# A recurrence with added filling products in every half step and in its head, and a head with its columns on a semaphore of their own

## The reference

```python
ms = jnp.mean(jnp.square(tokens), axis=-1, keepdims=True)
x = tokens * jax.lax.rsqrt(ms + EPS) * norm_w
x = x.reshape(B, T, H, D)            # 8, 256, 16, 8
a_t = jnp.tanh(a)                    # 16, 64, 64
def step(state, x_t):
    state = jnp.tanh(jnp.einsum('bhs,hst->bht', state, a_t) + jnp.einsum('bhd,hds->bhs', x_t, b))
    mixed = jnp.einsum('bhs,hsd->bhd', state, c) + skip[None] * x_t
    return (state, mixed)
_, outs = jax.lax.scan(step, state0, moveaxis(x, 1, 0))
return tokens + outs @ w_out.T + b_out
```

## Time and profile before

| | |
|---|---|
| time, median of 3 runs | 1920.63 us (1919.22 to 1922.42) |
| span of the profiled execution | 1914.6 us |
| mean granted clock of PE | 0.883 |
| PE busy | 1691.7 us (88%) |
| DVE busy | 1499.7 us (78%) |
| ACT busy | 1262.2 us (66%) |
| POOL busy | 453.8 us (24%) |

### The profile page before, as it was taken

One profiled execution on the slowest core, in us unless ns is written; L12 is line 12 of the kernel. 1 busy time (PEld: TensorE's weight loads), 2 busy tenths in 40 slices (PEclk: granted clock), 3 DMA queues, 4 the chain that ended last, 5 costly groups with the idle time before them and its releaser, 6 DMA issues. The chain is left out here.

```text
span 1914.6 us, 45800 instructions
## 1 busy us (share of the span) xinstructions
PE 1691.7 (88%) x16657; PEld 1055.0 (55%) x16662; DVE 1499.7 (78%) x3630; ACT 1262.2 (66%) x3371; POOL 453.8 (24%) x581
## 2 busy tenths in 40 slices
PE   5999977969869999966679999999969999999786
PEld 4999973437634444444444444444436666566453
DVE  4444457968779999978779999999967877788675
ACT  5666646856646655567558888888856666566675
POOL 1000001318411111110012222222214344435333
PEclk7555568969979999978789999999979999999998
DMA  3200005500024444200056666666610000000000
GB/s 80 91 4 4 4 13 196 190 1 2 2 98 157 156 163 169 106 1 1 1 206 234 224 222 231 233 226 222 230 61 23 12 11 23 23 2 1 1 11 15
DMA packets 52464, 174.80 MB, mean 91 GB/s; under 512 B 7376, under 2 KB 32976, under 8 KB 34896
## 3 DMA queue, kind: packets, MB, share of 16 engines
q1 hardware_dynamic: 51152, 170.69, 24.8%
q10 hardware_dynamic: 1152, 1.90, 0.3%
HBM read 168.05 MB, written 2.95 MB: 89 GB/s over the span
## 5 line engine op out<-in xcount | busy, mean ns | idle before, releaser
L864 DVE TENSOR_TENSOR ps<-ps,m_comb 128x512 f32<-128x512 f32 x520 | 363.0, 698 | 24.7 <-DMA m_comb<-m_shares 7.4
L849 DVE TENSOR_TENSOR m_hwlo<-ps,m_hwhi 128x512 f16<-128x512 f32 x520 | 353.6, 680 | 0.3
L825 ACT ACTIVATE m_hwhi<-ps 128x512 f16<-128x512 f32 x520 | 308.7, 594 | 20.9 <-DVE ps L864 19.5
L831 ACT ACTIVATE ps<-ps 128x512 f32<-128x512 f32 x388 | 225.8, 582 | 80.5 <-PE ps L781 80.4
L754 POOL CAST m_whi<-m_stage 128x256 f16<-128x256 f32 (+1 forms) x130 | 55.5, 427 | 899.9 <-PE ps L787 633.6
L781 PE MATMUL ps<-x_hi,m_whi 128*128 128x512 f16 x652 | 249.3, 382 | 11.1 <-DVE m_hwlo L849 6.6
L781 PE MATMUL ps<-x_lo,m_whi 128*128 128x512 f16 x652 | 249.1, 382 | 0.0
L781 PE MATMUL ps<-x_hi,m_wlo 128*128 128x512 f16 x652 | 248.9, 382 | 0.0
L463 DVE TENSOR_TENSOR rn_s_lo<-rn_s_full,rn_s_hi 128x32 f16<-128x32 f32 x512 | 98.5, 192 | 131.8 <-ACT rn_s_full L420 131.8
L787 PE MATMUL ps<-m_hwhi,m_whi 128*128 128x512 f16 x520 | 197.5, 380 | 0.3 <-DVE m_hwlo L849 0.2
L787 PE MATMUL ps<-m_hwlo,m_whi 128*128 128x512 f16 x520 | 197.3, 379 | 0.0
(11 more groups left out here) (456 smaller groups left out, 3973.2 us busy)
## 6 DMA issues: line engine op xcount, KB each, us to landing
m_comb<-m_shares SPq DMA_DIRECT2D x128, 1024.0 KB, 5.1
m_stage<-in_m_w SPq DMA_DIRECT2D x97, 128.0 KB, 4.5
m_stage<-in_m_w SPq DMA_DIRECT2D x33, 192.0 KB, 4.6
kept_lj_w<-in_lj_w SPq DMA_DIRECT2D x6, 1024.0 KB, 4.9
kept_lq_w<-in_lq_w SPq DMA_DIRECT2D x1, 1600.0 KB, 8.0
kept_la_w<-in_la_w SPq DMA_DIRECT2D x1, 1280.0 KB, 5.6
rn_rows<-in_L_attn_rows SPq DMA_DIRECT2D x4, 256.0 KB, 4.3
rn_xs<-rn_xn_hi SPq DMA_DIRECT2D x32, 32.0 KB, 1.9
```

Source lines behind the costliest of these rows:

```text
L825: nc.scalar.activation(hw_hi[:, k % HB, :], weighted(k), ACT.Copy).then_inc(hi_done, 1)
L831: nc.scalar.activation(acted(k), ps[:, 4, :] if gated else bank(k), func).then_inc(act_done, 1)
L849: nc.vector.tensor_tensor(hw_lo[:, k % HB, :], weighted(k), hw_hi[:, k % HB, :], ALU.subtract)\
L864: nc.vector.tensor_tensor(weighted(k), bank(k), comb[:, s, n * QW:(n + 1) * QW], ALU.mult)\
```

## The change

- The load of `cols` goes ahead of the later groups of rows and gets the semaphore `load_cols`. `base` on DVE and the scaling on ACT wait for it and no longer for w_out.
- ACT asks for the table of the square root at its start and for that of the tanh right after the square root. It scales group 0, then makes `at_hi` itself (a tanh to fp16) and `a_t`, then scales groups 1 to 3 to f32 only.
- POOL waits until the rows are normalised, then does what it did, and then the high and low parts of groups 1 to 3 of xn. DVE keeps the low part of group 0 and that of a.
- PE gets 3 products of 128x512 f32 between the raw and the normalised transposes, and 4 more ahead of the first injection (`exercise_rows`).
- Each half step but those of step 0 gets one more product between its filling products and its wait for `lo_done` (`exercise`): 2 x 192 columns in window 0 and in the first step of each window, 2 x 128 in all others. It writes into columns of banks 6 and 7 that nothing reads.

```diff
@@ -187,6 +187,7 @@
     NW = T // K
     W = GP * B
     HALF = N // 2
+    WARM = (3, 4)
     ps = S.psum
     with ExitStack() as ctx:
         def sb(name, shape, dt=F32):
@@ -221,7 +222,8 @@
 
         id_got, idb_got, a_got, b_got, c_got, o_got = S.sems.new(
             "load_ident", "load_identb", "rnn_a_got", "rnn_b_got", "rnn_c_got", "rnn_o_got")
-        kept_got = S.sems.new("kept_got")
+        kept_got, cols_got = S.sems.new("kept_got", "load_cols")
+        later_full, later_hi, later_lo = S.sems.new("rnn_later_full", "rnn_later_hi", "rnn_later_lo")
         kept = [name for name in S.kept if not name.endswith(("_hi", "_lo"))]
         rows_got = [S.sems.new(f"load_rows{g}") for g in range(4)]
         xs_got = [S.sems.new(f"rnn_xs_got{g}") for g in range(4)]
@@ -263,9 +265,9 @@
             rows_in = A["L0_attn_rows"].rearrange("i p c -> p i c")
             sp.dma_start(rows[:, 0:4, :], rows_in[:, 0:4, :]).then_inc(rows_got[0], 16)
             sp.dma_start(S.ident[:], A["c_ident"]).then_inc(id_got, 16)
+            sp.dma_start(cols[:], A["L0_attn_cols"]).then_inc(cols_got, 16)
             for g in range(1, 4):
                 sp.dma_start(rows[:, 4 * g:4 * g + 4, :], rows_in[:, 4 * g:4 * g + 4, :]).then_inc(rows_got[g], 16)
-            sp.dma_start(cols[:], A["L0_attn_cols"]).then_inc(o_got, 16)
             sp.dma_start(a_raw[:], A["L0_attn_a"]).then_inc(a_got, 16)
             sp.dma_start(b_w[:], A["L0_attn_b"]).then_inc(b_got, 16)
             sp.dma_start(c_w[:], A["L0_attn_c"]).then_inc(c_got, 16)
@@ -275,12 +277,18 @@
             hi_v, lo_v = [t[:].rearrange("p (r n) -> p r n", r=2) for t in (xn_hi, xn_lo)]
             for g in range(4):
                 cut = slice(g * 256, (g + 1) * 256)
-                sp.wait_ge(xhi_s, g + 1)
+                if g == 0:
+                    sp.wait_ge(xhi_s, 1)
+                else:
+                    sp.wait_ge(later_hi, g)
                 for q in range(4):
                     for copy in range(2):
                         sp.dma_start(xs_v[32 * copy:32 * copy + 32, q, :, cut], hi_v[32 * q:32 * q + 32, :, cut])\
                             .then_inc(xs_got[g], 16)
-                sp.wait_ge(xlo_s, g + 1)
+                if g == 0:
+                    sp.wait_ge(xlo_s, 1)
+                else:
+                    sp.wait_ge(later_lo, g)
                 for q in range(4):
                     sp.dma_start(xs_v[64:96, q, :, cut], lo_v[32 * q:32 * q + 32, :, cut]).then_inc(xs_got[g], 16)
             for name in kept:
@@ -291,6 +299,7 @@
         @block.gpsimd
         def _(pool):
             pool.wait_ge(b_got, 16)
+            pool.wait_ge(xr_s, 4)
             nc.gpsimd.tensor_copy(b_s[:], b_w[:]).then_inc(bhi_s, 1)
             pool.wait_ge(bhi_s, 1)
             nc.gpsimd.tensor_tensor(b_s[32:64], b_w[32:64], b_s[32:64], ALU.subtract).then_inc(b_s_done, 1)
@@ -299,15 +308,31 @@
             nc.gpsimd.tensor_copy(c_hi, c_w[:]).then_inc(chi_s, 1)
             pool.wait_ge(chi_s, 1)
             nc.gpsimd.tensor_tensor(c_lo, c_w[:], c_hi, ALU.subtract).then_inc(c_done, 1)
+            for g in range(1, 4):
+                pool.wait_ge(later_full, g)
+                nc.gpsimd.tensor_copy(by_parity(xn_hi, g), by_time(xnT, g)).then_inc(later_hi, 1)
+                pool.wait_ge(later_hi, g)
+                nc.gpsimd.tensor_tensor(by_parity(xn_lo, g), by_time(xnT, g), by_parity(xn_hi, g), ALU.subtract)\
+                    .then_inc(later_lo, 1)
 
         @block.tensor
         def _(pe):
+            def exercise_rows(bank):
+                nc.tensor.matmul(ps[:, bank, :], S.ident[:], rows[:, 0:4, :], start=True, stop=True, skip_group_check=True)
+
+            def exercise(w, n):
+                nc.tensor.matmul(ps[:, 6 + (w + 1) % 2, P:P + 2 * n].rearrange("p (r n) -> p r n", r=2), at_hi[:, 0, :],
+                                 xn_hi[:].rearrange("p (r n) -> p r n", r=2)[:, :, 0:n], start=False, stop=False,
+                                 skip_group_check=True)
+
             pe.wait_ge(id_got, 16)
             for g in range(4):
                 pe.wait_ge(rows_got[g], 16)
                 for j in range(4):
                     last = nc.tensor.transpose(ps[:, g, j * P:(j + 1) * P], rows[:, 4 * g + j, :], S.ident[:])
                 last.then_inc(raw_up, 1)
+            for _ in range(WARM[0]):
+                exercise_rows(7)
             for g in range(4):
                 pe.wait_ge(xr_s, g + 1)
                 for j in range(4):
@@ -334,7 +359,9 @@
                     last.then_inc(outs_ready, 1)
 
             pe.wait_ge(base_s, 4)
-            pe.wait_ge(xn_s, 4)
+            for _ in range(WARM[1]):
+                exercise_rows(0)
+            pe.wait_ge(xn_s, 1)
             pe.wait_ge(b_s_done, 1)
             pe.wait_ge(xs_got[0], 12 * 16)
             for g in range(2):
@@ -345,6 +372,7 @@
                         last.then_inc(mm_done[g], 1)
             pe.wait_ge(athi_s, 1)
             pe.wait_ge(atlo_s, 1)
+            pe.wait_ge(later_full, 3)
             for w in range(NW):
                 fill = []
                 if w < NW - 1:
@@ -376,6 +404,7 @@
                             for _ in range(-(-len(fill) // left)):
                                 what = fill.pop(0)
                                 what[0](*what[1:])
+                        exercise(w, 192 if w == 0 or k == 0 else 128)
                         pe.wait_ge(lo_done[g], t)
                         for c in range(GP):
                             n = g * GP + c
@@ -387,7 +416,7 @@
             pe.wait_ge(outs_used, NW - 2)
             for n in range(3 * NP):
                 project(NW - 1, n)
-            pe.wait_ge(o_got, 32)
+            pe.wait_ge(o_got, 16)
             for g in range(NQ):
                 pe.wait_ge(outs_used, 4 * g + 4)
                 nc.tensor.matmul(ps[:, g, :], w_o[:], outsT[:, g * QW:(g + 1) * QW], start=True, stop=True)\
@@ -395,6 +424,7 @@
 
         @block.scalar
         def _(act):
+            nc.scalar.preload_act_table_set("sqrt_and_others")
             for g in range(4):
                 act.wait_ge(rows_got[g], 16)
                 for i in range(4 * g, 4 * g + 4):
@@ -403,15 +433,18 @@
             act.wait_ge(sq_s, 1)
             act.wait_ge(eps_s, 1)
             nc.scalar.activation(sd[:], ms[:], ACT.Sqrt, bias=S.eps_ap(1e-4), scale=1.0 / C).then_inc(std_s, 1)
+            nc.scalar.preload_act_table_set("exp_and_others")
+            act.wait_ge(cols_got, 16)
+            act.wait_ge(rows_s, 1)
+            nc.scalar.activation(by_parity(xn_hi, 0), turned_rows(4), ACT.Identity, scale=norm_w).then_inc(xhi_s, 1)
+            nc.scalar.activation(by_time(xnT, 0), turned_rows(4), ACT.Identity, scale=norm_w).then_inc(xn_s, 1)
             act.wait_ge(a_got, 16)
+            nc.scalar.activation(at_hi, a_raw[:], ACT.Tanh).then_inc(athi_s, 1)
             nc.scalar.activation(a_t[:], a_raw[:], ACT.Tanh).then_inc(at_s, 1)
-            act.wait_ge(o_got, 32)
-            for g in range(4):
+            for g in range(1, 4):
                 act.wait_ge(rows_s, g + 1)
-                nc.scalar.activation(by_parity(xn_hi, g), turned_rows(4 + g), ACT.Identity, scale=norm_w)\
-                    .then_inc(xhi_s, 1)
                 nc.scalar.activation(by_time(xnT, g), turned_rows(4 + g), ACT.Identity, scale=norm_w)\
-                    .then_inc(xn_s, 1)
+                    .then_inc(later_full, 1)
             for t in range(T):
                 for g in range(2):
                     act.wait_ge(mm_done[g], t + 1)
@@ -424,7 +457,7 @@
             for i, e in enumerate(S.eps):
                 last = nc.vector.memset(S.epsilons[:, i:i + 1], e)
             last.then_inc(eps_s, 1)
-            dve.wait_ge(o_got, 32)
+            dve.wait_ge(cols_got, 16)
             for g in range(4):
                 dve.wait_ge(raw_up, g + 1)
                 nc.vector.tensor_scalar(by_time(base, g), turned_rows(g), 2.0, b_out, ALU.mult, ALU.add)\
@@ -437,18 +470,11 @@
                 if i % 4 == 3:
                     last.then_inc(xr_s, 1)
 
-            def xn_low(g):
-                dve.wait_ge(xn_s, g + 1)
-                nc.vector.tensor_tensor(by_parity(xn_lo, g), by_time(xnT, g), by_parity(xn_hi, g), ALU.subtract)\
-                    .then_inc(xlo_s, 1)
-
+            dve.wait_ge(xn_s, 1)
+            nc.vector.tensor_tensor(by_parity(xn_lo, 0), by_time(xnT, 0), by_parity(xn_hi, 0), ALU.subtract)\
+                .then_inc(xlo_s, 1)
             dve.wait_ge(at_s, 1)
-            nc.vector.tensor_copy(at_hi, a_t[:]).then_inc(athi_s, 1)
-            xn_low(0)
-            dve.wait_ge(athi_s, 1)
             nc.vector.tensor_tensor(at_lo, a_t[:], at_hi, ALU.subtract).then_inc(atlo_s, 1)
-            for g in range(1, 4):
-                xn_low(g)
 
             def outs(w):
                 dve.wait_ge(outs_ready, w + 1)
```

## The result

| | before | after |
|---|---|---|
| median of 4 runs each | 1919.93 us (1916.05 to 1922.42) | 2010.32 us (2009.51 to 2015.07) |
| ratio, 95% interval | | 1.0485 (1.047 to 1.05) |
| span of the profiled execution | 1914.6 us | 2007.7 us |
| mean granted clock of PE | 0.883 | 0.865 |

The changed kernel is 4.85% slower. That lies far outside the range on record (1901 to 1930 us) and within 5 us of the first rival, "it stays at 1.2 GHz", with its 2015 us. The clock did not rise.

The account below looks back on a forecast made before the run. The prediction took a loop through ACT, DVE and PE, 0.88 us a step, to bound the recurrence. Its terms, -7.5 + 10.7 + 1.3 + 1.7 - 2.5 = +3.7 us, gave 1924.3 us, range 1901 to 1930.

Parts of the forecast that it names:

- the first rival: Recurrence: PE stays at 1.2 GHz, half step 640 ns, window 20.7 us, +94 us in all, 2015 us; chance 0.20.
- Will the clock rise?: Recurrence: the added columns bring PE from 1.2 to 2.4 GHz within window 0; chance 0.67.
- Head: Before the recurrence: earlier cols and faster normalising (some 3.1 us) start the recurrence at 23.2 us, -7.5 us.
- Half step 465 ns: Recurrence at 2.4 GHz: PE needs 465 ns a half step, more than the loop's 440, and becomes the bound.
- POOL, +1.7 us: Start of the recurrence: splits moved to POOL overlap it by about 4 us and hold DVE's s_lo, +1.7 us.
- Tail, -2.5 us: After the recurrence: the last 24 projections and the output products run faster at 2.4 GHz, -2.5 us.
- Window 0, +1.3: First window of the recurrence: wider added products, with its first 4 to 7 us at 1.2 GHz, cost +1.3 us.
- the price of the windows: Windows 1 to 15 at 2.4 GHz: the added columns make a window 14.99 us against 14.26, together +10.7 us.
- The second rival: Recurrence at 2.4 GHz: the loop stays the bound, step 0.86 us, window 13.8 us, -14.4 us, 1906 us; chance 0.13.

Follow-up runs that it names:

- e9_paced: The changed kernel with ten f32 products instead of four before the first injection, POOL's splits moved to ACT and DVE, kept loads spread out: 1920.8 us, ratio 1.0016.
- e11_paced_no_bridge: e9_paced with the change's own four f32 products before the first injection instead of ten: 2015.04 us in one run.
- e3_head_bare: The changed kernel without the added product of the half steps and without the seven f32 products of the head: 1910.17 us, ratio 0.9961.
- e6_clean_bare: The changed kernel with POOL's splits moved to ACT and DVE, without the f32 products and the added product of the half steps: 1911.58 us, ratio 0.9962.
- e10_bare_paced: e3_head_bare with the 19 kept loads spread out over the windows: 1908.28 us, ratio 0.9958.
- e2_head_only: The changed kernel without the added product of the half steps, all seven f32 products of the head kept: 1911.32 us, ratio 0.9962.
- e8_clean_84: e5_clean_bridge with the added products cut to 2 x 84 columns (2 x 152 in window 0 and first steps): 1968.16 us, ratio 1.0266.
- e5_clean_bridge: The changed kernel with ten f32 products instead of four before the first injection and POOL's splits moved to ACT and DVE: 1997.38 us, ratio 1.0421.
- e7_clean_96: e5_clean_bridge with the added products cut to 2 x 96 columns (2 x 160 in window 0 and first steps): 1975.1 us, ratio 1.03.

## Why the prediction was wrong

**The step that failed** is "Will the clock rise?". It put the added columns between two known cases, products of 64 to 256 columns at 0.98 and 8-column products at 0.50, and took a rise within window 0 at 0.67 against 0.20. The runs showed 0.50 in all 16 windows instead, and with it a half step of 640 ns on PE where the forecast had 465. It asked one question where there were two. Holding: yes, in e9_paced from 24 to 264 us, with nothing but the change's own columns. Raising: no, in the changed kernel and in e11_paced_no_bridge, in 16 windows each. I had even worked out the gap ahead of the recurrence (idle from 18 to 23.2; it was 17.4 to 22.7) and the start at 1.2 GHz, and then counted on a rise for which no row spoke: the 15 windows marked full at 0.50 were in the prediction as evidence for the rival. The Trainium skill, page "TensorE: Matmul & The Clock Gate", Part 1, has an idle stretch bring the throttle back, which the rows at 18 to 22 us agree with, and sustained activity release it; but a PE marked busy for 330 us, half of whose time went to products of 128 and 256 columns (0.32 of each 0.64 us), stayed at 0.50; there the measurement decides.

**What followed from it** was sized right in the rival: half step 640 ns (640), window 20.7 us (20.69), windows 1 to 13 +84 (+83.2), the last two +11.6 (+11.8), window 0 +6.3 (+7.2), head -7.5 (-8.0), sum +94 (+93.1).

**The forecast's own terms**, against e9_paced, where its condition holds:
- Head: first injection at 22.70 in the changed kernel (23.2 forecast). Normalising 3.22 us with no long one (3.1). SP to injection 9.27 (9.3). The three f32 products ended at 12.0 (12.9 forecast). Right.
- Half step 465 ns: 464 by the sum of the rows at 107.42 to 107.88; eight high products 0.20 us; window 15.03 (14.99). The value taken for an 8-column product with its load, 25 ns from 18-column rows, was right.
- POOL, +1.7 us. In e3_head_bare window 0 takes 16.1 us (first activations 22.05 and 38.19), in e6_clean_bare, with the splits moved, 14.6 (23.38 and 37.97): 1.5 us; by the same measure it is 1.1 in e10_bare_paced and 0.5 in e2_head_only, which starts 2.6 us later than e3_head_bare. So the +1.7 was a little above the largest of these. In the changed kernel it cost nothing: window 0 takes 21.7 us there, with an s_lo of 0.61 us at 24.07 beside POOL, and 21.7 in e11_paced_no_bridge without POOL, because DVE has 0.45 us to spare in each half step of 0.64.
- Tail, -2.5 us: in e9_paced it was -1.1 (first transpose 8.8 us after the last s_hi, 9.9 before). This term was mis-sized: PE waits 0.65 us for the last s_lo, and the clock falls in the middle of the projections, to 0.50 between 266 and 268 us. The prediction counted on 2.4 GHz throughout.
- Window 0, +1.3: +0.8.

The agreement of +3.7 forecast and +3.9 measured is in part luck. e9_paced has no splits on POOL, so the +1.7 isn't in it; the tail gave 1.4 us less than forecast, the head 0.5 less (-7.0 by first activations), and its profile has 1.8 us more than that of the kernel before in the rest of the program, which the change doesn't touch. What is confirmed is the price of the windows: +11.0 us for windows 1 to 15 against +10.7. The account of the forecast holds in the main; its condition didn't.

**The second rival**, a loop bound at 0.86 us and 1906 us, fails on e8_clean_84: at 2.4 GHz, with PE not the bound, the step was 0.875 us.

## What to carry to other kernels

Before a clock is counted on, ask three things apart: what the stage would gain from it, whether the work holds it, and whether the work raises it once it is gone. The gain comes first: a stage bound by a loop through several engines, as here (0.87 us a step at either clock), can only lose by columns that are added for the clock, and the part of the change without them was 0.4% faster than the kernel before. If the clock must be held, go through PE's idle times one by one: bridging the wait for the first data, taking POOL's work away from beside DVE's and spreading a burst of loads moved the fall from before the recurrence to 28 us, to 62 us and past its end. And check the clock column against the pace of one product of known width before you build on it.

## What was not expected of the hardware

- The recorded clock can be wrong for hundreds of microseconds: 1.00 over the whole recurrence of e6_clean_bare, while its 128-column products kept the pace of 1.2 GHz, 105 ns each.
- The clock has a memory in this loop: the same half steps (12 products of 8 columns, one of 128, one of 256) ran for 240 us at 2.4 GHz in e9_paced and for 330 us at 1.2 GHz in e11_paced_no_bridge, the kernels differing by six f32 products, which fill 5 us of idling ahead of the recurrence. The second is a single execution.
- A single stall of 0.72 us in a PE otherwise marked full (e5_clean_bridge, 60.66) stands right ahead of the fall (0.56 between 62 and 64). So does a gap of 0.65 us at the end of e9_paced (0.50 between 266 and 268). In e7_clean_96 and e8_clean_84 the clock fell with no stall, so a stall isn't the only thing that precedes a fall.
- Loads that fill the DMA engines can stall PE although it needs none of their data: 0.51 and 0.72 us here, in e6_clean_bare two steps of 2.90 and 1.65 us instead of 0.88; in the changed kernel they did not. Spread over windows they cost next to nothing: no stall in e9_paced and e10_bare_paced, one of 0.22 us in e11_paced_no_bridge.
- The low clock hardly slows narrow products: eight of 8 columns with their loads take 0.20 us at 2.4 GHz (107.42 to 107.62) and 0.21 at 1.2; the 256 columns take 0.11 and 0.21.
